# The one-hots of a relational edge count, built with two strips interleaved

## The chip, the cores and the metric

The kernel runs on one core of one Trainium2 chip. The metric is the device time in microseconds (us) of one execution; the kernel before took 1624.51 us, the median of three runs (1622.56 to 1626.06).

## The reference

The graph has 3125 nodes with 128 features and 100,000 edges, sorted by destination, each with one of 8 relation types. Two blocks follow each other:

```python
# block 0: a two-layer GCN with self-loops and deg^-1/2 norms, gated and biased by a context
x = layernorm(x + (gcn(leaky_relu(gcn(x, W1)), W2) * gate + bias))
# block 1: a two-layer relational GCN, per layer:
xt  = einsum('nd,rde->rne', x, W)          # 8 relations
agg = segment_sum(xt[rel, src], dst)
x   = relu(agg + x @ SW + b)
x = layernorm(x_in + x)
```

## The kernel before, in words

Scatter and gather over edges are turned into matrix products. The kernel counts edges into matrices of small integers: for the GCN, how often source s has an edge to destination d; for the relational layers, the same with the relation added. A segment sum is then a product of features (split into three bf16 parts) with counts (f16).

**How counts are made.** Edges are sorted by destination, so an interval of 128 sorted edges, a strip (one edge on each of the 128 partitions), covers a pair of destinations, PAIR = 2. Each edge of a strip has two keys: a low key (0 to 127, the source's place inside its tile) and a cell key (for the relational counting 0 to 399: destination of the pair, relation, source tile; RCELLS = 400). Two one-hot matrices, edges by 128 low values and edges by 400 cells, are multiplied on TensorE, and the product (128 x 400) in PSUM is the strip's count. Edges that don't belong have keys that match no value.

**The relational counting.** There are 384 steps (MADE * HSTRIPS = 48 * 8), each with two strips. In a step k

- VectorE (`strip_hots(k)`, lines 1804 to 1814) makes the one-hots: two tensor_scalar instructions of 128 elements (L1809) and two of 400 (L1812), each comparing a row of numbers `cell_h` with the key of one strip, a per-partition f32 scalar in `rel_cols`. It waits until step k - 3 is counted (HOTS = 3 buffers in `hot_mem`), and then signals `rhots_ready`;
- TensorE (`count_rstrip(k)`, L1288 to L1299) waits for `rhots_ready` and for ScalarE's copy of step k - 2 (the first 12 steps: of step k - 1), and makes two products of 400 columns;
- ScalarE (`turn_counts`, L929) copies both PSUM banks in one instruction of 800 elements, transposed, into a buffer of counts, `blocks`. At the first step of a new buffer it also waits for the store of that buffer's former content to DRAM and for the sums that read it.

The counts are gathered in halves of 8 steps (32 destinations by 8 relations). Around these steps TensorE sums them in the first relational layer: `sum_product` (L1385), products of 512 columns, some 5 a step, and `add_message` (L1408), which adds rows gathered from a DRAM table for the later destinations; POOL fetches those rows by indirect DMA (L798), each two gathers held back until a certain step is counted (`rstrip_counted`). After the last product of a pair of halves VectorE copies the sums from PSUM (`copy_sums2`, L1917), and the next pair's first product waits for that. On VectorE's queue the copy stands behind the one-hots of the step before it. `node_onehots` (L1925) makes the one-hots of the gathered rows, once a slot of 8 gathers. The first 12 steps stand among the table products of the GCN's end (L1306 on TensorE, copies L1822 on VectorE and L939 on ScalarE).

**The other counting.** The GCN's counts are made earlier (24 to 239 us of the span) by `pair_hots` (L1665 to L1668): 16 strips at a time, with two tensor_tensor instructions, 8 * 128 * 2 and 8 * 50 * 2 elements. There two strips are innermost: the one-hots lie as [.., value, strip of two], the row of numbers is `each_h`, every number twice, and the keys are f16, repeated over the values by a stride of 0. TensorE reads every second element (L1119). `each_h` lies in `hot_mem` and is made by an iota on POOL at the start (L735), after `cell_h` (L733). The next instruction on POOL's queue after L737 is the first indirect DMA of the start (L741).

Of the kernel before, what the change touches and what calls it, by code (L numbers as in the profile page):

```python
# [6 lines left out]
P = 128  # L7
# [37 lines left out]
HOT_RING = 2  # L45
# [172 lines left out]
def gnn_kernel(nc, x, src, dst, rel, ctx_in, W1, b1, W2, b2, Wg, bg, Wb, w1, sl1, rb1, w2, sl2, rb2, out):  # L218
# [8 lines left out]
    with ExitStack() as stack:  # L227
        def sb(name, shape, dt=f32):
            return stack.enter_context(nc.sbuf_tensor(name, shape, dt))
# [24 lines left out]
        cell_h = sb("cell_h", [P, RCELLS], f16)  # L254
        rel_cols = sb("rel_cols", [P, 2, RSTRIPS])
# [32 lines left out]
        def carve(at, n):  # L288
# [13 lines left out]
        each_h = hot_mem[:, HOT_RING * (PAIR_COLS + 2 * CH * GKEYS):HOT_RING * (PAIR_COLS + 2 * CH * GKEYS) + 2 * P]\  # L302
            .rearrange("p (n e) -> p n e", e=2)
        rlow_hot = hot_mem[:, 0:HOTS * 2 * P].rearrange("p (u c n) -> p u c n", u=HOTS, c=2)
        rcell_hot = hot_mem[:, HOTS * 2 * P:HOTS * 2 * (P + RCELLS)].rearrange("p (u c n) -> p u c n", u=HOTS, c=2)
# [418 lines left out]
        def _(pool):  # L724
# [8 lines left out]
            nc.gpsimd.iota(cell_h[:, :], pattern=[[1, RCELLS]], base=0, channel_multiplier=0,  # L733
                           allow_small_or_imprecise_dtypes=True).then_inc(patterns_ready, 1)
            nc.gpsimd.iota(each_h[:, :, :], pattern=[[1, P], [0, 2]], base=0, channel_multiplier=0,  # L735
# [351 lines left out]
        def _(pe):  # L1087
# [119 lines left out]
            def rest_of(slow):  # L1207
# [80 lines left out]
                def count_rstrip(k):  # L1288
# [7 lines left out]
                    for c in range(2):  # L1296
                        last = nc.tensor.matmul(ps[:, strip_bank(k) + c, 0:RCELLS], rlow_hot[:, k % HOTS, c, :], rcell_hot[:, k % HOTS, c, :],  # L1297
                                                start=True, stop=True)
# [242 lines left out]
        def _(dve):  # L1541
# [186 lines left out]
            def rest_of(slow):  # L1728
# [75 lines left out]
                def strip_hots(k):  # L1804
                    u, first = k % HOTS, strip_pair(k)
                    if k >= HOTS:
                        dve.wait_ge(rstrip_counted, k - HOTS + 1)
                    for c in range(2):
                        nc.vector.tensor_scalar(rlow_hot[:, u, c, :], cell_h[:, 0:P], rel_cols[:, 0, first + c:first + c + 1], 0.0,  # L1809
                                                ALU.subtract, ALU.is_equal)  # L1810
                    for c in range(2):
                        last = nc.vector.tensor_scalar(rcell_hot[:, u, c, :], cell_h[:, :], rel_cols[:, 1, first + c:first + c + 1], 0.0,  # L1812
                                                       ALU.subtract, ALU.is_equal)
                    last.then_inc(rhots_ready, 1)
# [257 lines left out]
```

## Time and profile before

| | |
|---|---|
| median of the runs | 1624.51 us (1622.56 to 1626.06, 3 runs) |
| span of the profiled execution | 1840.2 us |
| time of that execution outside the span | not recorded |
| TensorE busy | 1562.5 us, 85% of the span |
| VectorE busy | 779.7 us, 42% |
| ScalarE busy | 520.8 us, 28% |
| POOL busy | 917.4 us, 50% |
| mean granted TensorE clock | 0.949 |

The profiled execution is 215.7 us longer than the median of the runs. Busy time is the time in which an engine has an instruction under way; a wait, and the issue of a DMA, do not count. A chain of waits goes back from the last instruction to what released it. In the rows further on a line L1809 is line 1809 of the kernel before, and PEld is TensorE's load of weights.

### The profile page before, as it was taken

The page shows a single profiled execution, that of the slowest core. Times are in us where ns is not written, and L with a number is a line of the kernel's source. Part 1 is how long each engine was busy: PE and PEld are TensorE (multiplying, and loading weights), DVE is VectorE, ACT ScalarE, POOL GpSimd, SP SyncE. Part 2 cuts the span into 40 slices and gives each one's busy share as a digit, 9 for nine tenths or more (in the row PEclk, how much of TensorE's full clock was granted, in tenths as well). Part 3 has the DMA queues.
Part 4 walks back from the last instruction along what each step waited for, and adds up shares of the span by engine and source line. Part 5 has one row for each costly group of instructions (what it writes and reads, how often), then busy time and mean ns, then how long its engine had stood idle before and what let it go on. Part 6 is the DMA issues. An engine that isn't in the chain of part 4 may idle for free.

```text
span 1840.2 us, 25393 instructions
## 1 busy us (share of the span) xinstructions
PE 1562.5 (85%) x9744; PEld 949.8 (52%) x9744; DVE 779.7 (42%) x2390; ACT 520.8 (28%) x749; POOL 917.4 (50%) x931
## 2 busy tenths in 40 slices
PE   1379989998578889988899787898888998889986
PEld 1365554444355556555565455554555655556545
DVE  7999961337345555555465654530010010001102
ACT  0464520015234435444354543420000000000000
POOL 6500000000566566666666665646666666666665
PEclk9999999999789899999899998998999999989988
DMA  4312331534443444544455443325555355555441
GB/s 124 103 73 90 127 162 72 195 129 185 155 141 134 151 156 165 189 163 159 151 182 179 157 157 122 113 82 189 186 192 189 123 190 188 190 189 178 172 148 47
DMA packets 67473, 275.85 MB, mean 150 GB/s; under 512 B 19988, under 2 KB 25854, under 8 KB 54676
## 3 DMA queue, kind: packets, MB, share of 16 engines
q1 hardware_dynamic: 37940, 213.87, 30.1%
q0 software_dynamic: 29408, 60.29, 12.1%
q8 instruction: 81, 1.33, 0.3%
q14 instruction: 44, 0.36, 0.1%
HBM read 153.70 MB, written 120.38 MB: 149 GB/s over the span
## 4 chain that ended last, share of the span: by engine, by line
PE 66%; DVE 14%; another core or an unknown queue 6%; issue 6%; DMA 3%; POOL 2%; ACT 2%; POOLq 0%; DVEq 0%; ACTq 0%
PE ps L1385 34%; DVE hot_mem L1667 8%; PE ps L1408 8%; PE ps L1263 7%; PE ps L1297 7%; PE ps L1449 2%; PE ps L1435 2%; PE ps L1306 2%; ACT blocks L929 2%; DMA node_id<-table_rel,edges 1%; POOL node_id L798 1%; DMA acc<-table_rel,edges 1%; DVE hot_mem L1812 1%; POOL acc L798 1%
## 5 line engine op out<-in xcount | busy, mean ns | idle before, releaser
L798 POOL DMA_INDIRECT node_id<-table_rel,edges x445 | 439.0, 987 | 608.0 <-DMA table_rel<-node_id 358.3
L798 POOL DMA_INDIRECT acc<-table_rel,edges x429 | 419.3, 977 | 257.5 <-issue 113.2
L1385 PE MATMUL ps<-blocks,raw 128*128 128x512 f16 x1500 | 456.5, 393 | 15.5 <-DVE xn L1917 12.5
L929 ACT ACTIVATE blocks<-ps 128x800 f16<-128x800 f32 x384 | 315.6, 836 | 342.3 <-PE ps L1297 200.0
L1385 PE MATMUL ps<-blocks,dinv 128*128 128x512 f16 x1200 | 399.3, 395 | 13.5 <-issue 12.8
L1809 DVE TENSOR_SCALAR hot_mem<-cell_h,rel_cols 128x128 f16<-128x128 f16 x768 | 165.6, 268 | 265.9 <-PE ps L1297 152.9
L1297 PE MATMUL ps<-hot_mem 128*128 128x400 f16 x768 | 198.8, 344 | 68.0 <-ACT blocks L929 47.5
L1408 PEld LDWEIGHTS ps<-raw,node_id 128*128 128x128 f32 x996 | 193.8, 200 | 97.7 <-issue 38.9
L1385 PE MATMUL ps<-blocks,edges 128*128 128x512 f16 x600 | 236.8, 395 | 7.9 <-issue 7.6
L1408 PEld LDWEIGHTS ps<-raw,acc 128*128 128x128 f32 x962 | 183.7, 197 | 85.4 <-issue 31.0
L1812 DVE TENSOR_SCALAR hot_mem<-cell_h,rel_cols 128x400 f16<-128x400 f16 x768 | 224.8, 333 | 0.0
L1385 PEld LDWEIGHTS ps<-blocks,raw 128*128 128x128 bf16 x1500 | 164.4, 116 | 110.7 <-issue 35.1
L1408 PE MATMUL ps<-raw,node_id 128*128 128x64 f32 (+14 forms) x996 | 168.0, 252 | 26.4 <-DMA node_id<-table_rel,edges 19.1
L1385 PEld LDWEIGHTS ps<-blocks,dinv 128*128 128x128 bf16 x1200 | 132.4, 115 | 105.2 <-issue 35.1
L1408 PE MATMUL ps<-raw,acc 128*128 128x64 f32 (+13 forms) x962 | 159.0, 250 | 16.7 <-DMA acc<-table_rel,edges 9.1
L1667 DVE TENSOR_TENSOR hot_mem<-hot_mem,edges 128x2048 f16<-128x2048 f16 x200 | 164.0, 885 | 10.7 <-remote 8.2
L1954 DVE TENSOR_TENSOR tin<-tin,xT 128x128 f32<-128x128 f32 (+3 forms) x16 | 5.9, 366 | 347.7 <-ACT tin L989 267.1
L1297 PEld LDWEIGHTS ps<-hot_mem 128*128 128x128 f16 x768 | 73.3, 108 | 152.1 <-ACT blocks L929 75.5
L1119 PE MATMUL ps<-hot_mem 128*128 128x50 f16 x1600 | 65.1, 195 | 57.2 <-DVE hot_mem L1667 41.6
L854 ACT ACTIVATE blocks<-ps 128x800 f16<-128x800 f32 x100 | 83.0, 837 | 73.2 <-PE ps L1119 61.8
L1119 PEld LDWEIGHTS ps<-hot_mem 128*128 128x128 f16 x1600 | 57.6, 103 | 88.2 <-ACT blocks L854 42.3
L982 ACT ACTIVATE raw<-ps 128x512 f32<-128x512 f32 x24 | 25.3, 1055 | 266.3 <-remote 155.6
(183 smaller groups left out, 1296.2 us busy)
## 6 DMA issues: line engine op xcount, KB each, us to landing
rcounts<-blocks SPq DMA_DIRECT2D x44, 1600.0 KB
blocks<-rcounts SPq DMA_DIRECT2D x44, 1600.0 KB
counts<-blocks SPq DMA_DIRECT2D x6, 3200.0 KB, 11.0
blocks<-counts SPq DMA_DIRECT2D x5, 3200.0 KB, 10.5
table_rel<-node_id SPq DMA_DIRECT2D x50, 256.0 KB, 2.1
table_rel<-xn SPq DMA_DIRECT2D x50, 256.0 KB
node_id<-table_rel,edges POOLq DMA_INDIRECT x445
acc<-table_rel,edges POOLq DMA_INDIRECT x429
```

The source lines that it names most:

```text
L798: nc.gpsimd.indirect_dma_start(got[m % GATHERS][:, j, :], None, tables_rel[layer - 2], bass.IndirectOffsetOnAxis(ap=row_i[:, first + j:fir ...
L854: nc.scalar.activation(block_of(b)[:, :, at:at + 2 * PAIR * CH].rearrange("p t (u n) -> p t u n", u=2), ps[:, 2 * (h % 2):2 * (h % 2) + 2, ...
L929: nc.scalar.activation(to.rearrange("p t (b m) -> p t b m", b=2), ps[:, strip_bank(k):strip_bank(k) + 2, 0:RCELLS].rearrange("p b (m t) -> ...
L1119: last = nc.tensor.matmul(ps[:, 2 * (h % 2) + c // CH, c % CH * GKEYS:(c % CH + 1) * GKEYS], low_hot[:, h % HOT_RING, c // 2, :, c % 2], c ...
L1263: nc.tensor.matmul(total, part, buffer_of(i)[:, t * n:(t + 1) * n], start=first, stop=False)
L1297: last = nc.tensor.matmul(ps[:, strip_bank(k) + c, 0:RCELLS], rlow_hot[:, k % HOTS, c, :], rcell_hot[:, k % HOTS, c, :], start=True, stop= ...
L1306: nc.tensor.matmul(ps[:, q % FAST_BANKS, :], xT[:, t * P:(t + 1) * P], wr1[:, 4 * h:4 * h + 4, :].rearrange("p r f -> p (r f)"), start=Tru ...
L1385: last = nc.tensor.matmul(ps[:, bank, 0:2 * HCOLS], part, half_pairs[u % 2][:, :, t * HCOLS:(t + 1) * HCOLS], start=(k == 0), stop=(k == T ...
L1408: last = nc.tensor.matmul(ps[:, GATHER_BANK, a - start_:b - start_], got[m % GATHERS][:, j, :], nodehot[:, m % ONEHOTS, j, a - base:b - ba ...
L1667: last = nc.vector.tensor_tensor(hot[:, u, :, :, :], each_h[:, 0:n, :].unsqueeze(1).to_broadcast([P, CH, n, 2]), keys.unsqueeze(2).to_broa ...
L1809: nc.vector.tensor_scalar(rlow_hot[:, u, c, :], cell_h[:, 0:P], rel_cols[:, 0, first + c:first + c + 1], 0.0, ALU.subtract, ALU.is_equal)
L1812: last = nc.vector.tensor_scalar(rcell_hot[:, u, c, :], cell_h[:, :], rel_cols[:, 1, first + c:first + c + 1], 0.0, ALU.subtract, ALU.is_e ...
```

## The change

The relational counting takes the layout of the other one. In a step the one-hots of both strips are made by one tensor_tensor for the low keys (128 * 2 elements) and one for the cells (400 * 2 elements), with the two strips innermost. `rel_cols` becomes f16; `each_h` becomes a tensor of its own with 400 numbers, each twice; `cell_h` keeps the 64 numbers that `node_onehots` reads. TensorE's weights and moving columns of the step are then every second element of `hot_mem`.

```diff
-        cell_h = sb("cell_h", [P, RCELLS], f16)
-        rel_cols = sb("rel_cols", [P, 2, RSTRIPS])
+        cell_h = sb("cell_h", [P, WIN], f16)
+        rel_cols = sb("rel_cols", [P, 2, RSTRIPS], f16)
+        each_h = sb("each_h", [P, RCELLS, 2], f16)
...
-        each_h = hot_mem[:, HOT_RING * (PAIR_COLS + 2 * CH * GKEYS):HOT_RING * (PAIR_COLS + 2 * CH * GKEYS) + 2 * P]\
-            .rearrange("p (n e) -> p n e", e=2)
-        rlow_hot = hot_mem[:, 0:HOTS * 2 * P].rearrange("p (u c n) -> p u c n", u=HOTS, c=2)
-        rcell_hot = hot_mem[:, HOTS * 2 * P:HOTS * 2 * (P + RCELLS)].rearrange("p (u c n) -> p u c n", u=HOTS, c=2)
+        rlow_hot = hot_mem[:, 0:HOTS * 2 * P].rearrange("p (u n c) -> p u n c", u=HOTS, c=2)
+        rcell_hot = hot_mem[:, HOTS * 2 * P:HOTS * 2 * (P + RCELLS)].rearrange("p (u n c) -> p u n c", u=HOTS, c=2)
...
-            nc.gpsimd.iota(cell_h[:, :], pattern=[[1, RCELLS]], base=0, channel_multiplier=0,
+            nc.gpsimd.iota(cell_h[:, :], pattern=[[1, WIN]], base=0, channel_multiplier=0,
...
-            nc.gpsimd.iota(each_h[:, :, :], pattern=[[1, P], [0, 2]], base=0, channel_multiplier=0,
+            nc.gpsimd.iota(each_h[:, :, :], pattern=[[1, RCELLS], [0, 2]], base=0, channel_multiplier=0,
...
-                        last = nc.tensor.matmul(ps[:, strip_bank(k) + c, 0:RCELLS], rlow_hot[:, k % HOTS, c, :], rcell_hot[:, k % HOTS, c, :],
+                        last = nc.tensor.matmul(ps[:, strip_bank(k) + c, 0:RCELLS], rlow_hot[:, k % HOTS, :, c], rcell_hot[:, k % HOTS, :, c],
...
-                    for c in range(2):
-                        nc.vector.tensor_scalar(rlow_hot[:, u, c, :], cell_h[:, 0:P], rel_cols[:, 0, first + c:first + c + 1], 0.0,
-                                                ALU.subtract, ALU.is_equal)
-                    for c in range(2):
-                        last = nc.vector.tensor_scalar(rcell_hot[:, u, c, :], cell_h[:, :], rel_cols[:, 1, first + c:first + c + 1], 0.0,
-                                                       ALU.subtract, ALU.is_equal)
+                    for hot, n, a in ((rlow_hot, P, 0), (rcell_hot, RCELLS, 1)):
+                        last = nc.vector.tensor_tensor(hot[:, u, :, :], each_h[:, 0:n, :],
+                                                       rel_cols[:, a, first:first + 2].unsqueeze(1).to_broadcast([P, n, 2]), ALU.is_equal)
                     last.then_inc(rhots_ready, 1)
```

## Rows read from the trace of the kernel before

**Rows 1.** Window: length, busy us (count) of PE, PEld, DVE, ACT, POOL; clock, DMA.

```profile
476.00:1216.00 740.00, 639.38 (x3537) 399.65 (x3536) 396.72 (x1594) 326.64 (x445) 459.46 (x459) 0.94 0.44 150
```

**Rows 2.** The chain of waits in 426 to 1216 us, by line.

```profile
by line: PE ps L1385 33.8%; PE ps L1297 16.6%; another core or an unknown queue 13.4%; PE ps L1408 8.9%; PE ps L1449 4.8%; ACT blocks L929 3.8%; issue 3.1%; PE ps L1435 2.6%; PE ps L1306 2.1%; DVE hot_mem L1812 2.1%; DVE hot_mem L1809 1.5%;
```

**Rows 3.** Timeline, a steady step: start us, us, engine, line, operation, tiles, count.

```profile
503.73 0.50 PE L1297 MATMUL ps<-hot_mem 128*128 128x400 f16 x2
504.07 0.59 PE L1385 MATMUL ps<-blocks,raw 128*128 128x512 f16 x2
...
505.46 0.50 PE L1297 MATMUL ps<-hot_mem 128*128 128x400 f16 x2
```

**Rows 4.** Groups in 476 to 1216 us: count, busy us, mean ns, idle before.

```profile
L1812 DVE TENSOR_SCALAR hot_mem<-cell_h,rel_cols 128x400 f16<-128x400 f16 x726 | 213.3, 335 | 0.0
L1809 DVE TENSOR_SCALAR hot_mem<-cell_h,rel_cols 128x128 f16<-128x128 f16 x726 | 157.1, 269 | 265.9 <-PE ps L1297 152.9 <-remote 83.1 <-issue 28.7
```

**Rows 5.** Timeline of VectorE, steps of one-hots that follow each other without a wait.

```profile
462.68 0.40 DVE L1809 TENSOR_SCALAR hot_mem<-cell_h,rel_cols 128x128 f16<-128x128 f16 x2
463.00 0.54 DVE L1812 TENSOR_SCALAR hot_mem<-cell_h,rel_cols 128x400 f16<-128x400 f16 x2
463.47 0.41 DVE L1809 TENSOR_SCALAR hot_mem<-cell_h,rel_cols 128x128 f16<-128x128 f16 x2
```

**Rows 6.** Groups of the whole span: the tensor_tensor pair of the other counting.

```profile
L1667 DVE TENSOR_TENSOR hot_mem<-hot_mem,edges 128x2048 f16<-128x2048 f16 x100 | 121.0, 1210 | 10.7 <-remote 8.2 <-PE ps L1119 2.3
L1667 DVE TENSOR_TENSOR hot_mem<-hot_mem,edges 128x800 f16<-128x800 f16 x100 | 55.9, 559 | 0.0
```

**Rows 7.** Timeline of VectorE: one such pair (2048 and 800), and what follows.

```profile
134.31 1.69 DVE L1667 TENSOR_TENSOR hot_mem<-hot_mem,edges 128x2048 f16<-128x2048 f16 x2
135.93 0.68 DVE L1694 TENSOR_TENSOR raw<-raw 128x512 bf16<-128x512 f32 x1
```

**Rows 8.** Timeline of TensorE: single columns (L1092), and every second of 100 (L1119).

```profile
11.06 2.40 PE L1092 MATMUL ps<-ones_h,blocks 128*128 128x1 f16 x84 [4.33 <-DVE blocks L1566]
...
165.31 0.58 PE L1119 MATMUL ps<-hot_mem 128*128 128x50 f16 x16
```

**Rows 9.** Timeline, the change from one pair of halves to the next.

```profile
512.39 0.42 DVE L1809 TENSOR_SCALAR hot_mem<-cell_h,rel_cols 128x128 f16<-128x128 f16 x2 [3.34 <-remote]
...
514.02 1.03 DVE L1917 COPY xn<-ps 128x512 f32<-128x512 f32 x1
...
515.20 0.59 PE L1385 MATMUL ps<-blocks,raw 128*128 128x512 f16 x1 [0.57 <-DVE xn L1917]
```

**Rows 10.** Timeline of TensorE, a step that waited for its one-hots.

```profile
770.80 0.50 PE L1297 MATMUL ps<-hot_mem 128*128 128x400 f16 x2 [1.59 <-DVE hot_mem L1812]
```

**Rows 11.** Waits in 426 to 1216 us: us in total, times, longest.

```profile
ACT blocks L929 <- remote: 93.1, 29, 6.8
```

**Rows 12.** Timeline of POOL beside VectorE: gathers next to tensor_tensor, and next to nothing.

```profile
57.07 9.81 DVE L1667 TENSOR_TENSOR hot_mem<-hot_mem,edges 128x2048 f16<-128x2048 f16 x12
...
61.03 1.31 POOL L741 DMA_INDIRECT acc<-in_dst,gather_at  x1 [0.30 <-issue]
...
464.02 1.28 POOL L798 DMA_INDIRECT node_id<-table_rel,edges  x1 [0.30 <-issue]
...
467.14 0.94 POOL L798 DMA_INDIRECT node_id<-table_rel,edges  x1 [0.30 <-issue]
```

**Rows 13.** Timeline of the start: POOL, and VectorE where it waits.

```profile
0.95 1.51 POOL L727 IOTA blocks<- 128x1664 f16 x1
3.02 0.47 POOL L733 IOTA cell_h<- 128x400 f16 x1
3.44 1.54 POOL L735 IOTA hot_mem<- 128x256 f16 x1
...
8.25 1.29 POOL L741 DMA_INDIRECT acc<-in_dst,gather_at  x1 [3.16 <-DVE gather_at L1574]
...
47.05 1.71 DVE L1667 TENSOR_TENSOR hot_mem<-hot_mem,edges 128x2048 f16<-128x2048 f16 x2 [3.98 <-remote]
```

## The prediction

> **What bounds the kernel now.** I read the windows first. The change touches one stretch, the relational counting, 426 to 1216 us of the span. In its main part, 740 us long, TensorE is busy 639 us, POOL 459 us, VectorE 397 us [rows 1]: TensorE is the engine that fills it, and VectorE, whose work is changed, is idle almost half of it. The chain of waits says the same by line: TensorE's sums L1385 33.8% and the counting products L1297 16.6%, then 13.4% of "unknown queue"; the one-hots L1812 and L1809 stand in it with 2.1% and 1.5% [rows 2], 3.6% of 790 us or 28 us. So the reader is to look not at how much VectorE saves, but at the few places where TensorE waits for it.
>
> The timeline of a steady step shows why they are few: the counting products start 1.73 us apart (503.73, 505.46) [rows 3], while one-hots that follow each other without a wait need 0.79 us a step (462.68 to 463.47) [rows 5]. VectorE is two steps ahead. Where TensorE stops, ScalarE mostly waited first, 93 us "remote" in 29 waits [rows 11]; by the kernel's waits that is the store of a half's counts or the sums that still read the buffer. No one-hot ends such a wait.
>
> **The new pair on VectorE.** The trace has the same instruction with the same innermost layout in the other counting: 2048 elements 1210 ns, 800 elements 559 ns [rows 6], so (1210 - 559) / 1248 = 0.522 ns an element. The pair takes 1.62 us from its start to the next instruction's (134.31 to 135.93) [rows 7]. The new pair has 256 + 800 = 1056 elements in place of 2848: 1.62 - 1792 * 0.522 / 1000 = 0.685 us. That is 0.79 - 0.685 = 0.105 us less a step, 40 us of VectorE over 384 steps. From the first start to the end of the last it was 463.54 - 462.68 = 0.86 us and becomes 0.685 + (0.559 - 0.485) = 0.76 us (0.485 is the cadence of 800 elements: 1.62 / 2 + (800 - 1424) * 0.522 / 1000); 0.10 us less. Nearly all of this lies beside TensorE's sums and is worth nothing there.
>
> A rule of the Trainium skill speaks against this part. The row shows two tensor_tensor instructions at 1.62 us for 2848 elements, which leaves 0.07 us an instruction beside the streaming [rows 6, 7]. The page "VectorE: DVE Perf Modes" (section "The perf-mode tier table") says that tensor_scalar on 16-bit data runs at four elements a cycle and tensor_tensor at two at most, and its errata section charges 58 cycles an instruction; estimated by that page a step goes from 4 * 58 + 264 = 496 cycles to 2 * 58 + 528 = 644, 0.15 us longer. The tiers agree with the trace, the fixed cost does not: 0.79 us measured is well above the page's 0.52 us for the old four [rows 5]. I go by the rows and keep the other as a rival.
>
> **Where it is on the path.** Two kinds of place.
>
> 1. The change from one pair of halves to the next. The copy L1917, for which TensorE's next sum waits, starts at 514.02, right after eight one-hot instructions (two steps) that began at 512.39, and TensorE waits 0.57 us for it [rows 9]. Of the 20 such copies of the stretch 9 stand right behind one-hots; in 7 of these the next sum begins as soon as the copy is done: 4 behind two steps, 3 behind one. The gain is 4 * 0.21 + 3 * 0.105 = 1.15 us. In the other copies VectorE had been idle before.
> 2. Steps that waited for their own one-hots, as the one at 770.80 [rows 10]. I count 12 in which the one-hots are the last to end. Four or five of them, 461 to 465 us, lead only into a wait of TensorE for the first gathered rows and give nothing. The 7 others give 0.10 to 0.21 us each, 1.1 us.
>
> Sum: 2.3 us less. Bounds: 0, if every gain is spent in the next wait for a store; and, if all one-hots of the chain gave their share, 28 us * 0.105 / 0.79 = 3.7 us.
>
> **The products.** TensorE now reads every second column. Its rows for that: 16 products of 50 columns with strided weights and strided columns in 0.58 us [rows 8]. The last product of a run goes on for 0.16 us after its slot (0.50 - 0.34) [rows 3], so they are (0.58 - 0.16) / 16 = 26 ns apart. A product of one column comes 2.40 / 84 = 28 ns after the one before [rows 8], so 26 ns is what any small product takes, and the stride is not seen. The counting products take (504.07 - 503.73) / 2 = 0.17 us for 400 columns now, 0.42 ns a column [rows 3]. Bounds: 0, or, if 26 ns were all columns, 0.52 ns a column: 768 * 400 * 0.1 ns = 31 us. I take 0, to which the one-column row is nearest. Below nothing there is no reason.
>
> **POOL.** A gather issued beside tensor_tensor takes 1.31 us, beside the old one-hots 1.28 us, beside nothing 0.94 us [rows 12]. Both forms hold it up, and about equally. POOL has room: 740 us less 459 us busy and 459 gathers' 0.30 us of issue leaves 143 us [rows 1, 12]. The first eight gathers of the stretch are the exception, TensorE waits for them; three of them lie beside one-hots [rows 12], and 3 * (1.31 - 1.28) is 0.1 us, while the one-hots end 0.5 us earlier. I take 0; bounds -0.3 and +1.
>
> **The start.** `each_h` grows from 256 to 800 elements. The iota that repeats each number took 1.54 us for 256, 6.0 ns an element, where one without repetition took 1.51 us for 1664, 0.9 ns [rows 13]. Bounds for the new one 0.7 and 4.8 us; the old one with the same pattern is nearest, 4.8. `cell_h`'s gets shorter by about 0.3 us. POOL is then done at 3.44 - 0.3 + 4.8 = 7.9 us, 8.1 with the short iota behind it, where its first gather started at 8.25 after 3.16 us of idling [rows 13]. With the 0.30 us that lie between two gathers it starts at 8.4, or, if waking takes as long as before, up to 9.1. What is late there counts, since VectorE later waits for these gathers (3.98 us at 47.05) [rows 13]. I take 0.4 us; bounds 0 and 1.
>
> The copies into f16 `rel_cols` (ScalarE, six in all, long before their use) and the separate tensor cost nothing.
>
> **Sum.** -2.3 + 0 + 0 + 0.4 = -1.9 us. The sum is made against the span of 1840.2 us. The median of the runs is 215.7 us less, so waits in the profile are longer than in a run; the places above are orders of instructions and should be there too, but some may be fewer. I subtract unscaled: 1624.5 - 1.9 = 1622.6 us. What a measurement of this kernel can tell from no change is about 0.2%, 3.2 us.
>
> **The rivals.**
>
> - *More of VectorE's saving counts.* The old one-hots took 269 and 335 ns on average, more than beside nothing (two of them in 0.40 and 0.54 us, started 0.16 and 0.235 us apart, are 0.24 and 0.305 us each) [rows 4, 5]; if that was POOL holding them and the new pair is held less, a step saves 0.105 + 2 * 0.03 + 2 * 0.03 = 0.22 us, a quarter. For the chain's 28 us [rows 2] that is 7 us, and halves are stored earlier. Time: 1624.5 - 7 + 0.4 = 1618. Against it: a large part of these 28 us is the walk back through one-hots that ran beside ScalarE's copy and ended with it.
> - *The gathers become the bound* (slower). A gather that meets tensor_tensor waits for its end, and now that is so in every step. It decides once the mean gather is 143 / 459 = 0.31 us longer [rows 1], what one gather in rows 12 shows (0.37 us) and not the mean of all. Where slots are uneven it would come sooner: some 10 us of waits at L1408, 1634. The page "GPSIMD Engine Reference" of the Trainium skill (section "Key points") names both 2-port modes and two SBUF inputs as contending with POOL; the trace agrees for both forms, with 1.28 and 1.31 us.
> - *The new pair is longer than the old four* (slower). If an instruction's fixed cost is that of the old ones, (0.79 - 0.275) / 4 = 0.13 us, with 0.275 us of streaming at twice the rate of rows 6, the pair takes 0.81 us; by the page's difference, 0.15 us more. Some 20 steps on the path make 3 us at most: 1624.5 + 3 + 0.4 = 1628. Rows 7 speak against it.
> - *The long iota holds up the start* (slower), because VectorE works beside it: with both slowed by half, 4.8 * 0.5 = 2.4 us on top of the 1 us, less the 2.3 gained: 1626.
> - *Strided columns cost* (slower): +31 - 2 = 1654.
>
> **Chances.** My forecast 0.46, more saving 0.30, gathers 0.08, longer pair 0.06, start 0.08, columns 0.02. Faster by over 0.2%: the first rival and the edge of my own, 0.32; within 0.2%: 0.46; slower: 0.22 with the edge of the start. The range leaves out the columns, half of the gathers' case and the far end of the first rival: 1614 to 1631.
>
> **What would show it.** The profile after should have one tensor_tensor of 256 elements at about 0.27 us and one of 800 at 0.56 us, 384 each, and 0.69 us from step to step where nothing is waited for; VectorE busy some 40 us less; products of 400 columns still 0.17 us apart; gathers in 476 to 1216 us at a mean near 1.00 us; an iota of 800 elements near 4.8 us and the first gather before 9.1 us. I am wrong if the counting products move apart, if L1408 waits for gathers, or if the time falls by more than 5 us, which would mean that one-hots sat on the path far more often in a run than in the profile.

## The result, and the profile after

The changed kernel takes 1633.97 us (median of 4 runs, 1632.66 to 1636.60) where the kernel before takes 1624.12 us in the same comparison (4 runs, 1622.56 to 1626.06): ratio 1.0059 [1.0045, 1.0074], 9.9 us slower. The forecast was 1622.6 us and no measurable difference; the time lies outside the range of 1614 to 1631.

One thing on chips has to be said first. The profile on which the prediction rests has a span of 1840.2 us although the kernel's runs took 1624.5 us. Later runs showed two kinds of chip: on two of them the kernel before takes 1850 and 1833 us, on others 1624 to 1628 us. By its span and its clock of 0.949 the profile on record is one of the first kind. A second profile of the same kernel, from a chip of the second kind (run b1_same below), has a span of 1623.2 us at a clock of 0.985; "before" below means this one wherever microseconds are set against those of after (span 1631.3 us, clock 0.988).

The page of after begins with the span and with each engine's busy time, share of the span and instructions:

```profile
span 1631.3 us, 24625 instructions
PE 1489.6 (91%) x9744; PEld 922.2 (57%) x9744; DVE 733.8 (45%) x1622; ACT 524.6 (32%) x749; POOL 927.9 (57%) x931
```

First, the part that was changed. The groups of after (count, busy us, mean ns, idle before) answer to [rows 4]:

```profile
L1808 DVE TENSOR_TENSOR hot_mem<-each_h,rel_cols 128x800 f16<-128x800 f16 x384 | 218.6, 569 | 0.0
L1808 DVE TENSOR_TENSOR hot_mem<-each_h,rel_cols 128x256 f16<-128x256 f16 x384 | 111.7, 291 | 210.2 <-PE ps L1296 210.0
```

Two instructions a step, 384 of each, at 0.569 and 0.291 us: as forecast. Seven steps that follow each other without a wait take 4.89 us (14 instructions, 455.06 us, below), 0.69 a step; 0.685 was forecast, from 0.79 in [rows 5].

Then the relational counting. The windows (start:end, length, busy us and count of PE, PEld, DVE, ACT, POOL; clock, DMA), of before and of after, from about the first gather of the stretch to the last count; they answer to [rows 1]:

```profile
455.00:1083.00 628.00, 604.88 (x3552) 387.78 (x3552) 404.27 (x1613) 333.71 (x449) 465.94 (x469) 0.99 0.53 182
```
```profile
457.00:1092.00 635.00, 607.45 (x3549) 383.52 (x3549) 351.68 (x875) 333.31 (x449) 478.68 (x469) 0.99 0.52 180
```

VectorE is busy 53 us less, where 40 were forecast, and the stretch is 7 us longer. POOL, with the same 469 instructions, is busy 13 us more. The chain of waits by line, 418 to 1091 us, of before and of after, answers to [rows 2]:

```profile
by line: PE ps L1385 47.6%; PE ps L1297 17.4%; PE ps L1408 12.6%; PE ps L1449 6.0%; PE ps L1435 2.7%; PE ps L1306 2.5%; DVE xn L1917 2.1%; issue 1.5%; POOL node_id L798 1.1%; DMA acc<-table_rel,edges 0.9%; DVE hot_mem L1812 0.8%; PE ps L143
```
```profile
by line: PE ps L1384 43.0%; PE ps L1296 16.7%; PE ps L1407 11.3%; PE ps L1448 5.5%; issue 3.4%; POOL node_id L797 3.2%; PE ps L1305 2.6%; PE ps L1434 2.4%; POOL acc L797 2.3%; DVE xn L1913 1.9%; DMA acc<-table_rel,edges 1.7%; DMA node_id<-t
```

Both rows break off. By the whole chain, whose pieces the trace gives, the one-hots had 8.4 us of it (L1812 5.2, L1809 3.2) and have 4.2 (L1808). The gathers on POOL went from 8.2 us (L798, both tiles) to 37.2 (the 3.2 and 2.3% of L797), and "issue" from 1.5 to 3.4%; nearly all of this growth lies where the chain runs through POOL from one gather to the next (2.9 us before, 14.6 after). TensorE's waits in 453 to 1095 us (total us, times, longest) say the same; before, then after:

```profile
PE ps L1408 <- DMA node_id<-table_rel,edges: 7.8, 1, 7.8
...
PE ps L1297 <- DVE hot_mem L1812: 3.3, 8, 0.9
...
PE ps L1408 <- DMA acc<-table_rel,edges: 2.3, 1, 2.3
```
```profile
PE ps L1407 <- DMA node_id<-table_rel,edges: 12.2, 2, 10.7
...
PE ps L1407 <- DMA acc<-table_rel,edges: 4.1, 4, 2.3
...
PE ps L1296 <- DVE hot_mem L1808: 1.3, 3, 0.7
```

Waits for one-hots fell by 2.0 us, waits for gathered rows grew from 10.1 to 16.3 us. The sum of the two profiles: the first gather of the stretch starts at 456.7 us in place of 454.7 (+2.0); from its start to the start of the stretch's last gather, the 469th, it is 635.2 us in place of 627.6 (+7.5); what comes behind gives back 1.4 us. That is +8.1 us of span, of the 9.9 us in the medians.

**Where the 2.0 us arise.** The timeline of the start of after (start us, us), answering to [rows 13]:

```profile
3.02 0.18 POOL L732 IOTA cell_h<- 128x64 f16 x1
3.15 4.48 POOL L734 IOTA each_h<- 128x800 f16 x1
...
10.91 1.30 POOL L740 DMA_INDIRECT acc<-in_dst,gather_at  x1 [3.17 <-DVE gather_at L1573]
...
4.67 2.99 DVE L1621 CAST firsts_f<-firsts_i 128x7 f32<-128x7 int32 x1
7.70 1.23 DVE L1565 TENSOR_SCALAR blocks<-blocks,firsts_f 128x128 f16<-128x128 f16 x7
```

The same cast in before:

```profile
4.66 0.34 DVE L1622 CAST firsts_f<-firsts_i 128x7 f32<-128x7 int32 x1
```

The iota is as long as forecast (4.48 for 4.8 us). But a cast of seven elements, started 1.5 us after it, takes 2.99 us and ends with it (7.66 and 7.63 us). In before it was the same on a smaller scale: there the iota ended at 4.98 us (3.44 + 1.54) and the cast at 5.00. What VectorE does behind the cast is late by that, the gather indices with it, and POOL idles for them as long as it had before (3.17 and 3.16 us), only 2.7 us later.

**Where part of the 7.5 us arise.** The timeline of after at the first gathers of the stretch:

```profile
455.06 4.89 DVE L1808 TENSOR_TENSOR hot_mem<-each_h,rel_cols 128x256 f16<-128x256 f16 x14
456.73 4.05 POOL L797 DMA_INDIRECT node_id<-table_rel,edges  x1 [358.10 <-DMA table_rel<-node_id]
461.09 0.94 POOL L797 DMA_INDIRECT node_id<-table_rel,edges  x1 [0.30 <-issue]
...
471.28 0.56 PE L1407 MATMUL ps<-raw,node_id 128*128 128x4 f32 x2 [10.68 <-DMA node_id<-table_rel,edges]
```

And of before:

```profile
454.75 1.18 POOL L798 DMA_INDIRECT node_id<-table_rel,edges  x1 [359.27 <-DMA table_rel<-node_id]
456.23 1.28 POOL L798 DMA_INDIRECT node_id<-table_rel,edges  x1 [0.30 <-issue]
...
466.95 0.56 PE L1408 MATMUL ps<-raw,node_id 128*128 128x4 f32 x2 [7.82 <-DMA node_id<-table_rel,edges]
```

A gather that takes 0.94 us alone takes 4.05 us: it was issued inside the unbroken run of 14 tensor_tensor instructions (455.06 to 459.95 us) and ended 0.83 us after the run did. Nothing was let through between two instructions of this run. That is no law of every run; in the unit counting of the same profile gathers get in once per pair of instructions, 1.62 us apart, as long as a pair is [rows 7]:

```profile
52.49 8.67 DVE L1666 TENSOR_TENSOR hot_mem<-each_h,edges 128x800 f16<-128x800 f16 x11
...
54.17 1.32 POOL L740 DMA_INDIRECT xT<-in_src,gather_at  x1 [0.30 <-issue]
55.79 1.32 POOL L740 DMA_INDIRECT acc<-in_dst,gather_at  x1 [0.30 <-issue]
```

From the first gather to TensorE's first product with its rows it is 14.6 us, where it was 12.2. Over the stretch, 121 of the 469 gathers take over 0.1 us more than the 0.943 of a free one, where 66 did, and the time beyond 0.943 us that all of them take grew from 24.2 to 37.5 us.

**And the products.** The instructions of the counting line as the view of one line gives them (count, shortest/median/longest ns), before and after:

```profile
L1297 PE MATMUL ps<-hot_mem x768: 329/332/541, 418.4 to 1081.3; 128*128 128x400 f16 x192
```
```profile
L1296 PE MATMUL ps<-hot_mem x768: 336/338/535, 421.2 to 1090.8; 128*128 128x400 f16 x192
```

The shortest and the median are 6 to 7 ns longer. In the trace the next product starts 177.5 ns after one of these where it was 169: 8.4 ns each, 0.021 ns a column or 5%, 6.4 us of TensorE over 768 products.

### The profile page after: what moved, and what is told of

The parts are those of the page before. It is cut to its first block, busy times and chain, and to the rows that moved or that the text cites. A ratio compares the mean times of both kernels' runs of the same rounds, so it can differ in the third digit from the quotient of the medians.

```text
span 1631.3 us, 24625 instructions
## 1 busy us (share of the span) xinstructions
PE 1489.6 (91%) x9744; PEld 922.2 (57%) x9744; DVE 733.8 (45%) x1622; ACT 524.6 (32%) x749; POOL 927.9 (57%) x931
## 4 chain that ended last, share of the span: by engine, by line
PE 71%; DVE 14%; POOL 5%; DMA 5%; issue 4%; ACT 1%; POOLq 0%; DVEq 0%; SPq 0%; ACTq 0%
PE ps L1384 37%; PE ps L1407 9%; DVE hot_mem L1666 9%; PE ps L1262 8%; PE ps L1296 7%; PE ps L1448 3%; POOL node_id L797 2%; POOL acc L797 2%; PE ps L1305 2%; PE ps L1434 2%; DMA acc<-table_rel,edges 2%; DMA node_id<-table_rel,edges 2%; DVE xn L1913 1%; POOL acc L740 1%; PE ps L1264 0%
## 5 line engine op out<-in xcount | busy, mean ns | idle before, releaser
L797 POOL DMA_INDIRECT node_id<-table_rel,edges x445 | 442.2, 994 | 498.7 <-DMA table_rel<-node_id 358.1
L797 POOL DMA_INDIRECT acc<-table_rel,edges x429 | 424.7, 990 | 154.7 <-issue 108.8
L1384 PE MATMUL ps<-blocks,raw 128*128 128x512 f16 x1500 | 438.2, 379 | 7.1 <-DVE xn L1913 6.4
L1808 DVE TENSOR_TENSOR hot_mem<-each_h,rel_cols 128x256 f16<-128x256 f16 (+1 forms) x768 | 292.4, 430 | 210.2 <-PE ps L1296 210.0
L1384 PE MATMUL ps<-blocks,dinv 128*128 128x512 f16 x1200 | 381.2, 381 | 0.0
L1407 PEld LDWEIGHTS ps<-raw,node_id 128*128 128x128 f32 x996 | 188.4, 195 | 90.6 <-issue 29.5
L1384 PE MATMUL ps<-blocks,edges 128*128 128x512 f16 x600 | 228.4, 381 | 0.0
L1407 PEld LDWEIGHTS ps<-raw,acc 128*128 128x128 f32 x962 | 176.6, 190 | 69.8 <-issue 13.2
L1384 PEld LDWEIGHTS ps<-blocks,raw 128*128 128x128 bf16 x1500 | 158.0, 111 | 99.8 <-issue 13.3
L1666 DVE TENSOR_TENSOR hot_mem<-each_h,edges 128x2048 f16<-128x2048 f16 x200 | 164.0, 902 | 0.9 <-PE ps L1118 0.6
L1118 PEld LDWEIGHTS ps<-hot_mem 128*128 128x128 f16 x1600 | 57.5, 103 | 82.5 <-issue 44.3
L1921 DVE TENSOR_TENSOR raw<-cell_h,edges 128x512 f32<-128x512 f16 (+1 forms) x110 | 73.5, 681 | 51.0 <-PE ps L1407 49.4
```

What stands on the lines that cost most here:

```text
L797: nc.gpsimd.indirect_dma_start(got[m % GATHERS][:, j, :], None, tables_rel[layer - 2], bass.IndirectOffsetOnAxis(ap=row_i[:, first + j:fir ...
L1118: last = nc.tensor.matmul(ps[:, 2 * (h % 2) + c // CH, c % CH * GKEYS:(c % CH + 1) * GKEYS], low_hot[:, h % HOT_RING, c // 2, :, c % 2], c ...
L1384: last = nc.tensor.matmul(ps[:, bank, 0:2 * HCOLS], part, half_pairs[u % 2][:, :, t * HCOLS:(t + 1) * HCOLS], start=(k == 0), stop=(k == T ...
L1407: last = nc.tensor.matmul(ps[:, GATHER_BANK, a - start_:b - start_], got[m % GATHERS][:, j, :], nodehot[:, m % ONEHOTS, j, a - base:b - ba ...
L1666: last = nc.vector.tensor_tensor(hot[:, u, :, :, :], each_h[:, 0:n, :].unsqueeze(1).to_broadcast([P, CH, n, 2]), keys.unsqueeze(2).to_broa ...
L1808: last = nc.vector.tensor_tensor(hot[:, u, :, :], each_h[:, 0:n, :], rel_cols[:, a, first:first + 2].unsqueeze(1).to_broadcast([P, n, 2]), ...
```

## The experiments

Three suspects, then: the long iota at the start, gathers held longer by tensor_tensor, and products with strided columns. Ratios are to the kernel before on the same chip, with the 95% interval.

### First set: each suspect alone (before: 1850.28 us)

b0_same is the kernel before itself.

> The kernel before, once more, for a profile without the long waits of the first one. All theories: ratio 1.000, within 0.2%. My theory (the changed kernel lost its 9.8 us in two places: VectorE's cast at the start held by the longer iota, 2.6 us; POOL's gathers held by the tensor_tensor one-hots, the rest) expects here a cast L1622 of 0.34 us, 12.3 us from the first gather L798 to the first L1408 (14.6 in the changed kernel), and gathers in the counting stage that are shorter on average and an earlier end of that stage by some 4 us. The rival (the strided columns or weights slow TensorE) expects gathers alike and shorter products of 400 columns here.

e1_iota_late keeps the change, but builds only the first 128 numbers of `each_h` (256 elements) at the start, and the others on POOL behind its wait for the edges:

```
- iota(each_h[:, :, :], pattern=[[1, RCELLS], [0, 2]], base=0)
+ iota(each_h[:, 0:P, :], pattern=[[1, P], [0, 2]], base=0)
...
+ iota(each_h[:, P:RCELLS, :], pattern=[[1, RCELLS - P], [0, 2]], base=P).then_inc(each_ready, 1)
```

> The changed kernel, but the iota at the start fills only the 128 numbers that it filled before, and the other 272 are written by a second iota on POOL when its wait for the edges is over (about 350 us), where VectorE has idle time. If the long iota costs the start 2.6 us: the cast L1621 takes 0.34 us again and the time falls from 1634 by 2.6 us, to 1631.4. If what was lost at the start is made good later (a stage not bound by VectorE): no change, 1634.

e2_pe_stride is the kernel before, with TensorE alone changed: it reads the old one-hots, which lie one strip behind the other, as if their strips lay innermost. The counts come out wrong by that; the instructions, their number and their shapes stay.

```
- rlow_hot[:, k % HOTS, c, :], rcell_hot[:, k % HOTS, c, :]
+ rlow_odd[:, k % HOTS, :, c], rcell_odd[:, k % HOTS, :, c]
```

> The kernel before with one thing changed: TensorE reads the counting step's weights and columns as every second element, as in the changed kernel; VectorE writes as before. (The counts are then wrong, nothing else depends on them in time.) If the stride costs TensorE nothing: 1624, ratio 1.000, and the two products 0.17 us apart. If it is the loss: up to 1634.

e3_low_tt makes only the low one-hots (TensorE's weights) by one tensor_tensor; the cells stay as before, with contiguous columns.

```
- for c in range(2): tensor_scalar(rlow_hot[:, u, c, :], cell_h[:, 0:P], ..., ALU.is_equal)
+ tensor_tensor(rlow_hot[:, u, :, :], each_h[:, :, :], low_cols[:, first:first + 2]..., ALU.is_equal)
```

> The kernel before with the low one-hots alone in the new form: one tensor_tensor of 256 elements (0.20 us to the next start) in place of two tensor_scalar (0.33 us); the cell one-hots stay two tensor_scalar of 400. If POOL's gathers are held by long runs of tensor_tensor without a gap: a run is now broken by tensor_scalar, the gathers are held less than in the changed kernel, and the time is 1624 or 1 to 2 us less, as VectorE saves 0.13 us a step. If any tensor_tensor in a step holds the gathers as the full pair does: 1628 to 1631.

Measured: b0_same 0.9986 [0.9959, 1.0014], e1 0.9997 [0.9971, 1.0024], e2 0.9995 [0.9971, 1.0019], e3 0.9985 [0.9950, 1.0021]. On this chip no kernel differs from the one before by more than its interval, and that takes 226 us longer than on the chip of the first comparison; the intervals reach to either side about half as far as the 0.6% that is looked for. As a test of times the set failed. Its profiles still served: in e1 the cast at the start takes 0.17 us in place of 2.99, its first gather of the stretch 4.15 us behind tensor_tensor, and in e2 the counting products are 178 ns apart, with weights and columns alone changed.

### Second set: the same on a chip of the second kind (before: 1625.85 us)

b1_same is before again, e4_iota_late is e1, e5_low_tt is e3. e6_cell_tt is e4 with the roles of e5 turned round: low one-hots by two tensor_scalar, cells by one tensor_tensor of 800, so that columns are strided and weights are not.

> The kernel before, for a profile on a chip where it takes 1624 us (the last comparison ran where it takes 1850 us, with pockets in which every engine stands still). All theories: ratio 1.000. My theory (the long iota holds VectorE's cast, tensor_tensor one-hots hold POOL's gathers) expects the cast L1622 at 0.34 us, 12.3 us from the first gather L798 to the first L1408 (14.6 after), and the gathers' excess over 0.943 us in the counting stage under 30 us in sum (37.5 us after).

> The changed kernel with the start's iota as short as before (128 numbers; the other 272 come at about 350 us). Where the kernel before takes 1624 and the changed one 1634: 1631.4 if the long iota costs the start 2.6 us and nothing makes it good, 1634 if it is made good later, 1624 if it is the whole loss. Where the kernel before takes 1850: within noise of it.

> The kernel before with the low one-hots alone as one tensor_tensor, the cell one-hots as two tensor_scalar. If POOL's gathers are held by tensor_tensor until it ends, and by a run of them until the run ends: the low one is short (0.29 us) and the run is broken, so 1622 to 1624, ratio 0.999 to 1.000 (of 1624). If any tensor_tensor in the step costs what the pair costs: 1628 to 1631.

> The opposite half: low one-hots by two tensor_scalar, cell one-hots by one tensor_tensor of 800 elements (0.57 us), the long iota taken out of the start as in the other experiment. If the hold is by single instructions, the long one holds the gathers most: 1628 to 1631, with the first gather under 1.6 us as the run is broken by tensor_scalar. If only the unbroken run matters: the first gather short and the time 1625 to 1627. If the loss is the strided reading: as the changed kernel, 1631.

Measured: b1_same 1627.22 us, 1.0011 [0.9999, 1.0022]; e4 1633.61, 1.0059 [1.0039, 1.0078]; e5 1623.98, 0.9993 [0.9983, 1.0002]; e6 1632.65, 1.0054 [1.0034, 1.0075].

A kernel measured against itself stands at 1.0011 here, so 0.1% is what two such numbers can differ by for no reason. The loss comes with the cells' half: e6 has all of it, e5 none. In e5, with strided weights and contiguous columns, the products are 169 ns apart, in e6 177.5: strided weights are free, columns are not. The lines of the products, e5 and e6:

```profile
L1297 PE MATMUL ps<-hot_mem x768: 329/332/541, 418.9 to 1077.4; 128*128 128x400 f16 x192
```
```profile
L1300 PE MATMUL ps<-hot_mem x768: 336/338/535, 418.2 to 1084.7; 128*128 128x400 f16 x192
```

In e6 the runs on VectorE are cut by tensor_scalar, and its first gather is not held for 4 us:

```profile
453.73 1.22 POOL L801 DMA_INDIRECT node_id<-table_rel,edges  x1 [165.70 <-DMA table_rel<-node_id]
```

From first gather to first product with its rows it is 12.5 us (12.2 in before). So the 4 us hold is no condition of the loss. e6 has both the long tensor_tensor and the strided columns, so this set can't tell these two apart. Gathers held over 0.1 us: 56 in e5, 111 in e6, 66 in b1_same. The group of the gathers (count, busy us, mean ns, idle before), in b1_same, then e5, then after:

```profile
L798 POOL DMA_INDIRECT node_id<-table_rel,edges x240 | 238.0, 992 | 440.1 <-DMA table_rel<-node_id 359.3 <-issue 58.5 <-PE ps L1297 21.5
```
```profile
L798 POOL DMA_INDIRECT node_id<-table_rel,edges x240 | 237.7, 990 | 437.8 <-DMA table_rel<-node_id 359.0 <-issue 62.3 <-PE ps L1297 15.8
```
```profile
L797 POOL DMA_INDIRECT node_id<-table_rel,edges x240 | 247.1, 1030 | 435.8 <-DMA table_rel<-node_id 358.1 <-issue 59.7 <-PE ps L1296 17.0
```

It is the tensor_tensor of 800 elements, 0.57 us long, that holds gathers: of the 141 gathers of after that take 1.0 us or more, 87 end 0.82 us after one of these does (a gather alone takes 0.94), 30 after a short one, and the other 24 after the tensor_tensor of `node_onehots` (L1921). tensor_scalar holds gathers in the same way: of the 84 that take 1.0 us or more in b1_same, 39 end 0.82 us after one of 400 elements (L1812), but such an instruction is 0.3 us long and a gather loses less by it. e4 was expected at 1631.4 us if the long iota costs 2.6; by its median it shows no gain from the mended start, although its cast takes 0.17 us and its first gather of the stretch comes at 453.6 us, 3.2 before that of after. That contradicts the next set, and I come back to it.

### Third set: the columns taken out again (before: 1627.86 us)

f1_pe_stride is e2. f2_after_flat is the change with TensorE reading as before, contiguously (`rlow_flat[:, k % HOTS, c, :]`, `rcell_flat[:, k % HOTS, c, :]`, views of the same bytes); f3_late_flat is that with the late iota. In f1, f2 and f3 the counts are wrong, as in e2, while the instructions keep their number and shapes. f4_after is the change itself.

> The kernel before, TensorE alone changed: it reads weights and columns of the counting step as every second element of what VectorE writes as before (the counts are wrong). Stride theory: the 400 strided columns take 177.5 ns to the next start in place of 169, as in the trace after; 768 times 8.4 ns is 6.4 us, ratio 1.0040. Hold theory (tensor_tensor holds POOL's gathers, the gathers pace the counting stage): no tensor_tensor was added, ratio 1.000.

> The changed kernel, TensorE alone put back: it reads each one-hot as a contiguous block of what VectorE now writes interleaved (the counts are wrong). Everything else as changed: both tensor_tensor, f16 keys, the long iota at the start. Stride theory: 6.4 us of the loss go, 2 to 3 us of the start stay, ratio to before 1.0015 to 1.002. Hold theory: the loss stays, 1.0055 to 1.006.

> As the one before, and the long iota taken out of the start too (128 numbers at the start, 272 later). What is left of the change is VectorE's pair of tensor_tensor. Stride theory: 1.000, or up to 0.001 less for the shorter one-hots, plus up to 2 us for the first gather that is held 4 us behind a run of them. Hold theory: 1.004 to 1.005. The difference to the run before it is the start: 2 to 3 us (0.0012 to 0.0018) or nothing.

> The changed kernel again, beside its variants on the same chip. All theories: 1.006 where the kernel before takes 1624 us; where it takes 1850 us, 1.000 to 1.004.

Measured: f1 1626.33 us, 0.9997 [0.9984, 1.0010]; f2 1633.67, 1.0040 [1.0024, 1.0055]; f3 1629.60, 1.0016 [1.0005, 1.0026]; f4 1635.15, 1.0047 [1.0034, 1.0061].

- f3 against before: the tensor_tensor pair, with the f16 keys and the second iota that it needs, costs 1.7 us by the medians, 2.6 by the ratio (0.8 to 4.2). That is little more than the 1.0011 at which b1_same stood against itself. The saving on VectorE is there in full (729.7 us busy for 784.4) and buys nothing.
- f2 against f3: the long iota alone costs 4.1 us (the two intervals only just touch; the profiled spans are 5.9 us apart, and the first gather of the stretch starts at 457.96 us in place of 453.89).
- f4 against f2: strided columns beside the other two, 1.5 us, inside the noise of the medians.
- f1 against before: strided columns alone, nothing. Yet its products are slower, exactly as in after; here are f1 and f3:

```profile
L1299 PE MATMUL ps<-hot_mem x768: 336/338/535, 418.5 to 1080.4; 128*128 128x400 f16 x192
```
```profile
L1301 PE MATMUL ps<-hot_mem x768: 329/332/541, 418.6 to 1084.1; 128*128 128x400 f16 x192
```

f1 has the longer products and ends its counting at the same time as before (1080.4 and 1081.3 us); f3 has the short ones and ends it 3 us later. From the first gather to the last counting product f1 and before take 626.5 us both, with TensorE busy 607.3 and 603.3: its idle time fell from 23.3 to 19.3 us. The longer products ate waits, mostly those for gathered rows (10.1 us before, 7.0 in f1). In f3 the idle time is 28.6 us. f3's first gather:

```profile
453.89 4.16 POOL L802 DMA_INDIRECT node_id<-table_rel,edges  x1 [165.47 <-DMA table_rel<-node_id]
```

From here to its first product with gathered rows it is 14.6 us as in after, 2.4 more than before. That is about what f3 loses; that it is this hold which makes the loss was not tried, and e6 loses without it.

### Fourth and fifth set: what covers the stride?

If f1's stride is free because POOL's gathers pace the stretch, it must cost once they pace it less. "less" leaves the eighth gather of each slot of that layer out (`min(chunks, CH - 1)` of them, with the counts of the semaphores reduced alike; TensorE multiplies what lies where the rows would be): g1 and h1 are the kernel before so, g2 and h2 f1, g3 f3. g4 is e1 once more.

> The kernel before without the eighth gather of each slot in the counting stage (TensorE multiplies the rows that lie there; output wrong). It is the base of the two runs that follow. If POOL's gathers pace the stage (606 us of its 628 are POOL's instructions and their 0.30 us of issue), an eighth fewer gathers shorten it until TensorE paces it: 10 to 20 us less than the kernel before, ratio 0.988 to 0.994. If TensorE paces it already: 1 to 3 us less.

> The same with TensorE reading every second element. The strided columns take 8.4 ns more each product, 6.4 us in all, which in the full kernel cost nothing by itself. If that was because POOL paced the stage: here 4 to 6.4 us more than the run before (ratio to before up by 0.0025 to 0.004). If the 8.4 ns are hidden in another way: no difference.

> The same with VectorE's pair of tensor_tensor, TensorE reading contiguous blocks, short iota at the start: what the hold of the gathers costs when POOL has room. In the full kernel this was 1.7 us (ratio 1.0016). If the hold costs because POOL paces the stage: here 0 to 1 us more than the first of these runs, the first gather's 4 us included or not, since TensorE waits for the first rows in any case, at most 2.3. If one-hots themselves cost: 1.7 us or more.

> The changed kernel with the short iota at the start, again, beside these. In two earlier comparisons it stood at 1.0059 (four runs) and the changed kernel at 1.0059 and 1.0047, though the traces give the iota 2.7 to 4 us and two variants that differ in it alone gave 4.1 us. If the iota costs what these say: 1.0025 to 1.004 here. If it is absorbed when the columns are strided: 1.005 to 1.006.

> The kernel before without the eighth gather of each slot of the counting stage, again: the first time it ran where the kernel before takes 1833 us, and took 64 us less. Where the kernel before takes 1624 us: if POOL paces the stage there too, 10 to 20 us less (as far as TensorE's 600 us of work allow); if TensorE paces it, 1 to 3 us less.

> The same with TensorE reading every second element. If the strided columns (6.4 us of TensorE's time) are hidden in the full kernel because POOL paces the stage, they show here: 4 to 6.4 us more than the run before. If not, no difference, within 1.5 us.

The fourth set fell on a chip of the first kind (before: 1833.41 us): g1 1769.57 us, 0.9694 [0.9652, 0.9736]; g2 1766.10, 0.9650 [0.9619, 0.9682]; g3 1768.36, 0.9662 [0.9630, 0.9693]; g4 1829.50, 0.9983 [0.9959, 1.0007]. There an eighth fewer gathers take 64 us off, and stride or pair make no difference that intervals of 6 to 8 us to either side could show. It isn't POOL's own time that bounds the stretch on that kind of chip: in b0_same POOL is busy 474 us of 750 and issues for 140. What grows there is a wait for transfers. ScalarE's copy of the counts waits for a queue that the profile can't name ("remote"); by the kernel's waits that is the store of a half's counts (total us, times, longest; 426 to 1216 us; b0_same, then g1):

```profile
ACT blocks L929 <- remote: 110.4, 33, 6.9
```
```profile
ACT blocks L933 <- remote: 44.4, 15, 6.9
```

The two are of different chips of this kind; g4, on g1's chip and with all gathers, has 82.5 us. In b1_same and h1 no such wait is in the stretch. With fewer gathers these waits shrink; why they are there on some chips only, no run shows. That they covered what the first set looked for is likely, and not shown.

On the second kind (before: 1624.95 us): h1 1619.44 us, 0.9967 [0.9955, 0.9979]; h2 1624.61, 0.9998 [0.9989, 1.0007]. With fewer gathers the stride costs 5.2 us, near the whole 6.4 that the products are longer; with all gathers it cost nothing (f1). So the gathers do cover it. But the gathers' own share was overrated: 10 to 20 us were expected of h1, and 5.5 came; TensorE, busy 601 of the 621 us that the stretch then takes, leaves little more. The two stand close together: in before, POOL is busy 466 us of the 628 and takes 0.30 us of issue for each of 468 instructions, 606 us together; TensorE is busy 605.

## Why the prediction was wrong

The sum was -2.3 us for the one-hots, 0 for the products, 0 for POOL and 0.4 for the start. In the third set the loss of 7.3 us (f4 against before) splits into 4.1 for the start (f2 against f3), 1.7 for the pair with all its gain on VectorE (f3 against before) and 1.5 for the columns beside the other two (f4 against f2). The terms that failed are the three that were put at nothing or nearly so; the start is the largest by these medians.

- **VectorE.** Right in the sizes of the step and of its instructions: 0.69 us a step, 0.29 and 0.57 us an instruction, 384 each. Its yield was put at 2.3 us, half at the copies between pairs of halves and half at steps that waited for their one-hots. TensorE's waits did fall, for L1917's copy from 7.8 to 6.4 us and for one-hots by 2.0. Nothing of that is seen in the time of f3.
- **POOL, a step that failed: "I take 0; bounds -0.3 and +1".** It compared single rows, 1.31 us beside tensor_tensor and 1.28 beside tensor_scalar [rows 12], and concluded that both forms hold a gather about equally. These rows show how long one gather is held by one instruction. They don't show how often that happens (66 against 121 of the gathers of the stretch) nor what an unbroken run of the new, shorter instructions does (4.05 us); the row beside tensor_tensor came from the other counting, where a gather is held for one instruction only. Measured with products and start as before: +1.7 us (f3). The rival "the gathers become the bound" named the mechanism and the sign, even the 1634 us; its size came about through three causes, not through this one.
- **The start, failed too: "I take 0.4 us; bounds 0 and 1".** It priced POOL's own queue and let VectorE go on beside the iota. What counted was a cast of seven elements that waited for the iota's end, and it is VectorE that makes the indices of POOL's first gather: 2.7 us later there, 2.9 at the first product of the unit counting (28.5 for 25.6 us). The rival of the start had this coupling, with "both slowed by half" in place of a full stop. Worth 4.1 us by f2 and f3, where 0.4 was taken and 1 was the bound.
- **The products, failed in the size: 0, with a row that could not tell.** Strided products of 50 columns go at 26 ns and those of one column at 28 [rows 8]; a cost of 0.021 ns a column, 1 ns on 50 columns, can't be seen there. The products took 6.4 us more of TensorE in place of 0; the bound of 31 us held that easily. What it cost the kernel was nothing beside the old one-hots (f1) and 1.5 us beside the new (f4 against f2). The trace agreed with the forecast in one point only: strided weights cost nothing.
- **What bounds the stretch.** "TensorE is the engine that fills it" was half of it. The room of 143 us on POOL came from a profile on a chip where everything stood still in pockets ("unknown queue", 13.4% of the chain [rows 2]); by the clean profile POOL's 606 us of 628 leave 22. With that number the gathers' rival would have begun to bite not at 0.31 us more a gather but at 22 / 468 = 0.05. Measured were 38 ns on the 240 gathers into `node_id` (1030 - 992) and 18 on the other 229, 27 on average: less than the room even so. The mean doesn't decide it; the chain runs through the gathers at single places, such as the first one.

Left open: the 2 by 2 of start and columns doesn't add up by the times. Iota late and columns flat is 1.0016 (f3), iota early 1.0040 (f2), columns strided 1.0059 (e4), both 1.0047 and 1.0059 (f4 and the first comparison). Taken through f2 the iota costs 4 us and the columns 1.5; taken through e4 the columns cost 7 and the iota nothing. The profiled spans (f3 1627.2, e4 1629.2, f2 1633.1, f4 1634.0) side with the first, but are one execution each, and e4's is of the shortest of its four (1631.01 us, the others up to 1637.38). The first gather of the stretch starts at 453.6 to 453.9 us in e4, e6 and f3 and at 456.7 to 458.0 in after, f2 and f4, so the late iota does bring its 3 to 4 us in e4 too; where its median lost them again, no trace shows. g4 was to settle this beside the others, and fell on a chip of the first kind. The stretch itself, from its first gather's start to its last's, is 3.3 to 4 us longer with strided columns in both pairs (631.3 to 635.3, 631.7 to 635.0), which fits e4. That columns cost nothing beside tensor_scalar and something beside tensor_tensor could be because TensorE's slower counting and POOL's held gathers delay each other in turn, so that neither covers the other; that is only argued. The split of the loss between pair and columns stays open by as much.

The version with the low half alone (e3, e5) is the best of the new ones, 0.9993 [0.9983, 1.0002]: clearly better than the change, not clearly better than the kernel before.

## What to carry to other kernels

Fewer and longer VectorE instructions need not be a gain where GpSimd gathers beside them: count how many gathers will meet a long tensor_tensor and look for unbroken runs, not at one pair of rows. Add up busy time and issue of every engine against the stretch before calling one of them free, and do it on a profile whose span agrees with the runs. Ask of a long one-time constant at the start which engines work beside it, and whether it can be built where its engine idles anyway.

## What the runs showed of the hardware

- A VectorE cast of seven elements beside a GpSimd iota took 2.99 us in place of 0.34 or 0.17: it ended 0.03 us after the iota. With the shorter iota of before it took 0.34 and also ended 0.02 us after it; where the iota ended at 4.69 us, right after the cast's start, it took 0.17 (e4).
- A gather that meets tensor_tensor, or tensor_scalar of 400 elements, ends 0.82 us after VectorE's instruction does (after, b1_same). Behind the unbroken run of 256 and 800 elements it waited for the end of the whole run (4.05 to 4.16 us in four kernels, 0.94 alone); behind the run of 800 and 2048 it got in at each pair (1.32 us). What makes the difference was not tried. The Trainium skill's "GPSIMD Engine Reference" (section "Key points") names the contention, and the trace agrees; that it can last through a run only these rows show.
- Moving columns at a stride of two f16 cost 5% at 400 columns (169 to 177.5 ns), strided weights nothing (e5).
- The same program took 1624 to 1628 us on some chips and 1833 to 1850 us on others, with 110 us of ScalarE's waits for transfers in the stretch of the latter (b0_same) and none on the former. An eighth fewer gathers took 64 us off there, 5.5 us on the others.
